# Softplus of the scans by a logistic function and squares on ACT, and an even spread of layer 0's scan groups

## The reference

```python
delta = jax.nn.softplus(jnp.einsum('er,brl->bel', dt_proj_w, dt_lo) + dt_proj_b[None, :, None])
def step(state, xs):
    d_t, B_t, C_t, u_t = xs
    dA = jnp.exp(d_t[..., None] * A)
    state = state * dA + (d_t * u_t)[..., None] * B_t[:, None, :]
    return (state, jnp.einsum('ben,bn->be', state, C_t))
```

## Time and profile before

| | us |
|---|---|
| median of 3 runs | 1293.16 |
| traced execution | 1297.12 |
| its span | 1295.4 |
| DVE busy in the span | 865.3 (67%) |
| POOL busy | 714.8 (55%) |
| PE busy | 1076.4 (83%) |
| ACT busy | 667.6 (52%) |

### The profile page before, as it was taken

How to read it: one execution, slowest core, us unless ns; L and a number is a source line. 1 busy time by engine, 2 the same in 40 slices (tenths; PEclk the granted TensorE clock), 3 DMA queues, 4 the chain that set the end, 5 groups by cost and what they waited for, 6 DMA issues and landing times.

```text
span 1295.4 us, 17796 instructions
## 1 busy us (share of the span) xinstructions
PE 1076.4 (83%) x5382; PEld 836.0 (65%) x5382; DVE 865.3 (67%) x1521; ACT 667.6 (52%) x1702; POOL 714.8 (55%) x480
## 2 busy tenths in 40 slices
PE   6576688778748878999999999798999737999992
PEld 3455577667514656888888888665555536887881
DVE  3885899878778975666656666769997772322221
ACT  4475355445462225778777777477652234333330
POOL 1106888888623223444454454439995206888873
PEclk8888799998968998999999999889999768999996
DMA  6494889986540003011101110304444983555555
GB/s 186 147 187 123 219 249 306 250 260 143 84 127 0 1 18 122 16 57 50 53 20 51 56 46 1 102 19 134 150 138 97 286 202 73 83 83 83 84 80 130
DMA packets 141119, 146.20 MB, mean 113 GB/s; under 512 B 34180, under 2 KB 127356, under 8 KB 141028
## 3 DMA queue, kind: packets, MB, share of 16 engines
q1 hardware_dynamic: 115556, 110.71, 29.5%
q0 software_dynamic: 24384, 33.31, 15.3%
q10 hardware_dynamic: 1088, 1.05, 0.2%
HBM read 119.04 MB, written 25.99 MB: 112 GB/s over the span
## 4 chain that ended last, share of the span: by engine, by line
PE 44%; POOL 18%; issue 14%; DVE 13%; DMA 6%; ACT 5%; another core or an unknown queue 0%; SPq 0%; ACTq 0%; POOLq 0%; DVEq 0%
PE bank L1629 4%; PE bank L1692 4%; PE bank L1725 4%; PE bank L1714 4%; POOL f_sums L1050 4%; POOL arena L1036 4%; PE bank L2491 3%; DMA f_sums<-arena,put 3%; POOL y L2407 2%; PE bank L1618 2%; PE bank L2159 2%; PE bank L1647 2%; PE bank L1703 2%; POOL arena L586 2%; DMA e_sums<-ctxT,put 2%
## 5 line engine op out<-in xcount | busy, mean ns | idle before, releaser
L566 DVE TENSOR_TENSOR_SCAN arena<-arena 128x1024 f32<-128x1024 f32 x64 | 155.2, 2425 | 15.4 <-issue 9.4
L1050 POOL DMA_INDIRECT f_sums<-arena,put x64 | 124.4, 1943 | 26.2 <-issue 17.1
L586 POOL TENSOR_TENSOR arena<-arena 128x1024 f32<-128x1024 f32 x32 | 82.5, 2577 | 89.6 <-DVE arena L566 89.6
L1036 POOL DMA_INDIRECT arena<-y_rows,slots x64 | 84.5, 1320 | 66.3 <-DVEq L1253 45.9
L2398 POOL DMA_INDIRECT e_sums<-ctxT,put x63 | 100.0, 1588 | 26.6 <-issue 16.2
L2491 PE MATMUL bank<-arena,ssm_y 128*128 x504 | 110.4, 363 | 0.9 <-issue 0.3
L544 ACT ACTIVATE arena<-arena,ssm_A 128x255 f32<-128x255 f32 x256 | 107.9, 499 | 1.1 <-DVE arena L488 0.9
L2159 PE MATMUL bank<-yT,arena 128*128 128x512 f32 (+1 forms) x224 | 104.3, 610 | 3.3 <-ACT arena L2090 3.3
L596 PE MATMUL bank<-arena,ident 128*128 128x256 f32 x256 | 68.7, 416 | 34.6 <-DVE arena L586 32.1
L2673 DVE TENSOR_SCALAR ctxT<-bank,slot_w 128x256 f32<-128x256 f32 x63 | 30.5, 484 | 99.1 <-DMA e_sums<-ctxT,put 89.5
L555 DVE TENSOR_TENSOR arena<-arena 128x1024 f32<-128x1024 f32 x64 | 94.3, 1473 | 0.2 <-DMA arena<-bc_rows 0.2
(11 more groups left out here) (342 smaller groups left out, 2777.1 us busy)
## 6 DMA issues: line engine op xcount, KB each, us to landing
arena<-bc_rows SPq DMA_DIRECT2D x64, 512.0 KB
arena<-in_L_ffn_w_gate_dram SPq DMA_DIRECT2D x16, 256.0 KB
arena<-in_L_ffn_w_up_dram SPq DMA_DIRECT2D x16, 256.0 KB
arena<-in_L_ffn_w_down_dram SPq DMA_DIRECT2D x16, 256.0 KB
x<-in_L_ffn_w_gate_dram SPq DMA_DIRECT2D x16, 256.0 KB
y<-in_L_ffn_w_up_dram SPq DMA_DIRECT2D x16, 256.0 KB
yT<-in_L_ffn_w_down_dram SPq DMA_DIRECT2D x16, 256.0 KB
arena<-in_L_ffn_Wd_dram SPq DMA_DIRECT2D x1, 3072.0 KB, 17.9
```

The lines of the kernel that those rows point to most:

```text
L566: nc.vector.tensor_tensor_scan(ssm_h[:, j % 2, :], ssm_decay[:, j % 2, :], ssm_in, 0.0, ALU.mult, ALU.add).then_inc(s_ssm_h, 1)
L586: ops.tensor_tensor(ssm_hC_buf[:, j % 2, :], ssm_h[:, j % 2, :], ssm_C[:, g % 2, :], ALU.mult).then_inc(s_ssm_hC, 1)
L1036: nc.gpsimd.indirect_dma_start(out=f0_xg[:, n % RING, e, :], out_offset=None, in_=y_rows, in_offset=bass.IndirectOffsetOnAxis(ap=slots[:, ...
L1050: nc.gpsimd.indirect_dma_start(out=f0_sums[m % SUMS], out_offset=bass.IndirectOffsetOnAxis(ap=put[:, m:m + 1], axis=0), in_=f0_ye[:, n % R ...
```

## The change

Softplus is computed another way. s is the logistic function: e / (2 + e) = sigmoid(-|z| - ln 2). The quartic in w is written as the product of two quadratics, each a square plus a constant: 2 atanh(s) = (du + near_add) x (t + 2 k far_add) x s, where du and t are squares that ACT makes of w with a bias from memory. ACT does Abs, Sigmoid and three squares for each block of 512 columns, DVE four operations for each half.

z goes through ACT once for all four blocks (`ssm_lin_act`, Identity with bias, followed by both products of u and D) ahead of the loop. The new `ssm_dt_act` then stands behind `silu(0)` for c = 0 and behind `silu(1)` for c = 1, each for two blocks. DVE's parts stand in pairs 1 and 2, and the groups from pair 3 on, one for each pair with a second one in pairs 3, 12 and 22. For the second scans `ssm_lin_act` comes ahead of the gate's Silu, ACT's blocks come in steps 0 to 3 of the feed-forward loop, DVE's parts in its steps 3 and 5, and `ssm_dt_done` in layer 2's attention.

```diff
+        def ssm_lin_act(act, m):
+            for c in range(HC):
+                for h in range(2):
+                    act.wait_ge(s_sp_dtp, 4 * m + 2 * c + h + 1)
+                    nc.scalar.activation(ssm_lin[:, c, h * HALF:(h + 1) * HALF], ssm_bank(2 * c + h)[:, :], ACT.Identity,
+                                         bias=ssm_par[:, 1, m, c:c + 1]).then_inc(s_sp_e, 1)
+            for c in range(HC):
+                nc.scalar.activation(ssm_y[:, m, :, c, :], ssm_u[:, c, :].rearrange("p (b l) -> p b l", b=B), ACT.Copy,
+                                     scale=ssm_par[:, 2, m, c:c + 1])
+
+        def ssm_dt_act(act, m, c, h):
+            cols = slice(h * HALF, (h + 1) * HALF)
+            lin, s, w = (z[:, c, cols] for z in (ssm_lin, ssm_e, ssm_w))
+            act.wait_ge(s_f0_const, 1)
+            act.wait_ge(s_sp_e, 8 * m + 4 + 2 * c + h)
+            act_link(nc.scalar.activation(s, lin, ACT.Abs))
+            act_link(nc.scalar.activation(s, s, ACT.Sigmoid, scale=-1.0, bias=soft_c[:, 0:1]))
+            act_link(nc.scalar.activation(w, s, ACT.Square))
+            nc.scalar.activation(ssm_du[:, c, cols], w, ACT.Square, bias=soft_c[:, 1:2])
+            nc.scalar.activation(ssm_delta[:, c, cols], w, ACT.Square, scale=math.sqrt(2 * SERIES),
+                                 bias=soft_c[:, 2:3]).then_inc(s_sp_e, 1)
...
+            dve.wait_ge(s_sp_e, 8 * m + 4 + 2 * c + 2)
+            dve_link(V.scalar_tensor_tensor(out=t, in0=t, scalar=2 * SERIES * far_add, in1=s, op0=ALU.add, op1=ALU.mult))
+            dve_link(V.scalar_tensor_tensor(out=t, in0=du, scalar=near_add, in1=t, op0=ALU.add, op1=ALU.mult))
+            dve_link(V.scalar_tensor_tensor(out=t, in0=lin, scalar=0.0, in1=t, op0=ALU.max, op1=ALU.add))
+            dve_link(V.tensor_tensor(du, t, u, ALU.mult))
...
+        f0_work = [[] for n in range(PAIRS)]
+        for c in range(HC):
+            f0_work[c + 1].append(("dt", 0, c))
+        for q in range(GROUPS):
+            f0_work[HC + 1 + q * (PAIRS - HC - 1) // GROUPS].append(("group", q // TURN, q % TURN))
...
             act.wait_ge(s_f0_clear, 16 * CLEARS)
-            ssm_dt_act(act, 0, 0)
+            ssm_lin_act(act, 0)
             step(0, 0, 0)
             for n in range(PAIRS):
                 if n + 1 < PAIRS:
                     step(n + 1, (n + 1) % RING, (n + 1) % 2)
                 silu(n, n % RING, n % 2)
-                if n == 0:
-                    ssm_dt_act(act, 0, 1)
+                if n < HC:
+                    for h in range(2):
+                        ssm_dt_act(act, 0, n, h)
                 if n:
                     evict(n - 1, (n - 1) % RING, (n - 1) % 2)
...
+                if i < 2 * HC:
+                    ssm_dt_act(act, 1, i // 2, i % 2)
...
-                for c, part in parts[2 + i:3 + i]:
-                    ssm_dt_part(dve, 1, c, part)
+                if i in (3, 5):
+                    ssm_dt_dve(dve, 1, (3, 5).index(i))
                 add(i)
...
-            ssm_dt_act(act, 1, 0)
+            ssm_lin_act(act, 1)
             gated_act(act, 0, 2)
-            ssm_dt_act(act, 1, 1)
             l1_act(act)
```

More of the change, by code:

```diff
@@ L462, in ssm_bc_sp, with ssm_dt_dve @@
                          x_dbl[DR:, :].rearrange("n (b l) -> n b l", b=B)).then_inc(s_sp_bc, 16)
-        def ssm_dt_dve(dve, m, c, part):
+        def ssm_dt_dve(dve, m, c):
             V = nc.vector
[L467 to L483, removed]
+            lin, s, t, du, u = (z[:, c, :] for z in (ssm_lin, ssm_e, ssm_delta, ssm_du, ssm_u))
+            dve.wait_ge(s_sp_e, 8 * m + 4 + 2 * c + 2)
[3 more added lines that the diff above has]
+            dve_link(V.tensor_tensor(du, t, u, ALU.mult))
+            if m == 0 and c == HC - 1:
                 ssm_dt_done(dve)
@@ L933, in flamingo_kernel @@
         s_f0_x = sem("s_f0_x")
-        f0_work = [[("dt", c, part) for part in range(3)] for c in range(HC)]
-        todo = [w for c in range(HC) for w in f0_work[c]] + [("group", q // TURN, q % TURN) for q in range(GROUPS)]
-        cost = [(6.5, 6.9, 3.7)[w[2]] if w[0] == "dt" else 4.75 for w in todo]
-        share, spent, f0_work = sum(cost) / PAIRS, 0.0, [[] for n in range(PAIRS)]
-        for n in range(PAIRS):
-            while todo and (spent + cost[0] / 2 <= share * (n + 1) or n == PAIRS - 1):
-                if f0_work[n] and todo[0][0] == "group" and todo[0][2] == 0 and n < PAIRS - 1:
-                    break
-                f0_work[n].append(todo.pop(0))
-                spent += cost.pop(0)
+        f0_work = [[] for n in range(PAIRS)]
[3 more added lines that the diff above has]
+            f0_work[HC + 1 + q * (PAIRS - HC - 1) // GROUPS].append(("group", q // TURN, q % TURN))
         f0_groups = [[w[1:] for w in work if w[0] == "group"] for work in f0_work]
@@ L1466, in add @@
                 norm_stats(dve, (i,), s_l1_x, i + 1)
-            parts = [(c, part) for c in range(HC) for part in range(7)][0:L1_PARTS]
-            for c, part in parts[0:2]:
-                ssm_dt_part(dve, 1, c, part)
             choose(0)
@@ L1928, in x_dve @@
             krms(0)
-            late = [(1, part) for part in range(L1_PARTS - 7, 7)]
-            for c, part in late[0:3]:
-                ssm_dt_part(dve, 1, c, part)
             qrms(0)
-            for c, part in late[3:]:
-                ssm_dt_part(dve, 1, c, part)
             ssm_dt_done(dve)
```

39 lines of the change are left out of this document (9 added, 30 removed).

## The result

The changed kernel takes 1306.2 us (median of 4, 1304.6 to 1307.9) where the kernel before takes 1293.0 beside it: ratio 1.0093, 95% interval 1.0064 to 1.0123. It is slower by 12 us (8 to 16). The forecast was 1292.4, with 1284 to 1300 around it.

A forecast was written before the change was run, and what follows sets the result against it. POOL's unbroken gathers and scatters were taken to bound layer 0's expert stage, DVE by busy share. Stage +1.2, gate -2.2, loop -1.0, Exp +1.3 sum to -0.7, giving 1292.4 us after subtracting the profiled run's 3.96 excess; range 1284 to 1300.

The forecast's parts named there:

- Late start, +6.5: Layer 0's expert stage: four softplus halves on ACT ahead of evict(0) make the first scatter 6.5 us later.
- First three pairs, +1.5: Layer 0, POOL: DVE's new operations and early scans make the first three pairs 7.9 us each, +1.5 us.
- Next 22 pairs, -2.1: Layer 0, POOL: fewer DVE operations holding POOL up over the next 22 pairs, -2.1 us, half of a possible -4.
- The tail, -4.7: Layer 0, closing scatters: the 4.68 us wait beside the last B and C loads goes, -4.7 us.
- Gate, -2.2: Layer 1's gate: Silu starts 2.2 us earlier, as its table load is no longer needed there.
- Loop, -1.0: Layer 1's feed-forward loop: DVE's softplus pieces cost 13.2 us in two lumps instead of 14.2, -1.0 us.
- Layer 2's first Exp, +1.3: Layer 2's attention: the first Exp needs a table load after the sigmoid set, +1.3 us.
- Rival 1: Layer 0: late first scatter is kept, POOL's tail gives nothing back; +4.0 us, 1297 (1299 with ACT's pause); chance 0.27.
- Rival 2: Layer 0: DVE's relief shortens POOL's pairs, 6.6 us beyond the sum, 1285.8; chance 0.31.
- Rival 3: ACT: Sigmoid, Tanh and Exp switch table sets, up to four more loads, 5 us, 1297.5; chance 0.04.
- the stage's upper bound: Layer 0's expert stage, summed at +1.2: +8 if the closing wait stays and nothing is won in between.

The follow-up runs named there:

- late_only: The kernel before plus only a delay: seven copies of 1.14 us on ACT ahead of evict(0); 1304.5 us, ratio 1.0071.
- l1_only: The kernel before with only the new softplus of the second scans (layer 1's loop), layer 0's stage as before; 1291.3 us, ratio 0.9978.
- spread_only: The kernel before with the old softplus and only the scan groups spread evenly over pairs 6 to 31; 1291.8 us, ratio 0.9983.
- after_again: The changed kernel as it is, measured and traced a second time; ratio 1.0071.
- exp_early: Changed kernel with ACT's blocks behind evict in pairs 0 to 3, DVE's second-softplus operations one by one, one early small Exp; 1286.6 us, ratio 0.9921.
- evict_first: The changed kernel with evict(n - 1) ahead of ACT's two blocks in pairs 0 and 1, nothing else; ratio 1.0029, repeated 1.0058.

## Why the prediction was wrong, point by point

**Late start, +6.5: right in mechanism, small in size.** Measured +7.1: the four blocks took 13.6 us and not 13.0 (from 113.46 to 129.12, less 1.28 for the load and 0.74 for the copy and Tanh between them). That POOL passes it on was right too, and late_only shows it alone: 8.25 us of delay made +6.4 at the first scatter (its trace has not the pause of 1.76) and 9 us in the time.

**First three pairs, +1.5: right.** 23.3 in both traces, 22.2 before: +1.1.

**Next 22 pairs, -2.1: wrong or too small to see.** 176.5 and 177.3, after 178.6 and 177.6: -1.2.

**The tail, -4.7: the step that failed.** I read the wait of 4.68 as the price of B and C rows beside the scatters, and took it as won whole. It did go, in all traces of the changed kernel. But the stretch from scatter 25 to the end is 31.8 in the mean where it was 32.8: -1.0. The groups that used to run while POOL waited now run beside the closing scatters, whose twelve durations sum to 23.8 and 25.0 where they were 21.8 and 20.9. The DVE timeline of the changed kernel beside the scatters of 341.13 and 346.64:

```profile
340.81 2.29 DVE L540 TENSOR_TENSOR_SCAN arena<-arena 128x1024 f32<-128x1024 f32 x1
...
346.32 2.29 DVE L540 TENSOR_TENSOR_SCAN arena<-arena 128x1024 f32<-128x1024 f32 x1
```

I had the rule for this myself, that scans hold POOL up, and didn't apply it to the moved groups. Nor is the wait tied to the order of the groups: l1_only has no such wait with the old order, and its last stretch is 30.5. spread_only has none either, and its stretch is 33.0, as long as before's with the wait. The Trainium skill (GPSIMD Engine Reference, Key points) gives that rule of the shared interface; the trace agrees with it once more (3.34 us beside each of the two scans above, 1.56 undisturbed).

**From the last scatter to the first sum: a term left out.** The prediction let everything behind the stage start when the last scatter has landed. ACT's own load of the third sum is a second path to the same point, as shown with the marks: 11.3 and 11.4 us after, 7.7 and 11.9 before, +1.5 in the mean. With such a spread in the kernel before, how much of it is the change's stays open.

**Gate, -2.2: right.** From the first sum of x to Silu 15.2 and 15.5 before, 13.0 and 12.4 after; over all traces the mean is 15.4 with the old gate (14.9 to 16.2) and 13.3 with the new one (12.0 to 15.2).

**Loop, -1.0: nearly right where PE's clock is the same.** The lumps of 6.6 us came as priced (rows below, the answer to the earlier trace rows).

```profile
450.59 1.21 DVE L482 SCALAR_TENSOR_TENSOR arena<-arena 128x1024 f32<-128x1024 f32 x1
451.83 2.83 DVE L483 SCALAR_TENSOR_TENSOR arena<-arena 128x1024 f32<-128x1024 f32 x1
...
455.96 1.22 DVE L485 TENSOR_TENSOR arena<-arena 128x1024 f32<-128x1024 f32 x1
```

From the first `add` to the last it is 65.6 us twice before, 67.5 and 65.0 after; the mean of the eight traces with lumps is 65.6, that of the five with the old loop 66.3: -0.7. From Silu to the last `add`, the stretch that the marks have, it is 104.8 twice before, 108.8 and 103.6 after. What sets these two apart is the speed of PE in the same program. PE's rows at the end of the loop, in the trace of 108.8:

```profile
466.03 1.97 PE L1372 MATMUL bank<-ident,arena 128*128 128x128 f32 x8 [3.55 <-POOL arena L1462]
...
485.66 1.84 PE L1372 MATMUL bank<-ident,arena 128*128 128x128 f32 x8 [2.84 <-POOL arena L1462]
488.67 5.68 PE L1379 MATMUL bank<-arena 128*128 128x256 f32 x16 [1.16 <-ACT arena L1402]
```

In after_again the last two took 1.09 us (behind a wait of 1.47) and 3.72, as before; and the loop's first product with the vectors took 7.13 us there, 9.46 in the trace of 108.8 (granted clock 0.50 from 403 to 407). Together that is 5.0 of the 5.2 us. The lumps don't bring the slow out-projection by themselves: six of the eight traces with lumps have 3.72, while two of the five with the old loop have 5.4 and all three with single operations 6.4 to 6.5, behind a wait of 2.36.

**Layer 2's first Exp, +1.3: right**, at the operation named (L1840, now L1809), on ACT's timeline, the answer to the earlier trace rows. From the last `add` to the second `x_kve` it is 31.7 and 30.6 after, 29.5 twice before.

```profile
521.12 1.28 ACT L1809 ACT_TABLE_LOAD   x1
522.41 0.56 ACT L1809 ACTIVATE arena<-bank,x_nb,x_rq 128x256 f32<-128x256 f32 x1
```

On the table load the trace stays with 1.28 us and the next operation at once, here and at 114.10. The Trainium skill's 1.38 us of drain on top (ScalarE: Activation LUTs, What ACT_TABLE_LOAD costs) isn't there.

**The rivals.** Rival 1, the late start kept, was the case, with 1297 for it where 1306 came: it kept the other gains. Its reason was off: the wait did go, and the closing scatters got longer instead. Rival 2 is out (mean scatter 1965 ns, gather 1313). Rival 3 is out: one load of the logistic set in layer 0 and one of Exp's at the first scan.

**The sum.** The marks give, in means of two traces each: start +7.1, first three pairs +1.1, next 22 -1.2, tail -1.0, first sum +1.5, gate -2.6, loop +1.4 and Exp with what follows +1.6, together +7.8 at the second `x_kve`, where the forecast had -0.7. The tail alone is 3.7 of the 8.5 us between them, the largest piece. From the first gather to the end of the span it is +5.9, so 2 us come back behind that mark; which of the later stages gives them, I didn't follow. The four traced executions themselves lie 6.9 us apart (1307.9 and 1300.0, 1297.1 and 1297.0). The timings say 9 to 12: after_again's trace is of the fastest of its six executions (median 1306.8), and the trace on which the forecast rests was 4 us slower than that kernel's median. So 2 to 5 us of the difference lie in executions of which there is no trace, and stay open.

The range was too narrow by its own terms as well: the stage's upper bound was +8, and with the gate and the loop at 0 and the Exp at 1.3 the bounds reach +9.3, 1302.5. Rival 1, on which the range ended, put the stage at +5.9, which is what the marks show at the end of the last scatter. The time of 1306 lies beyond even those bounds.

## What to carry to other kernels

What stands in a queue ahead of the first item of a saturated engine is paid about whole, whatever it relieves elsewhere: here the order of two calls on ACT was worth some 5 us, and a pure delay of 8 us on ACT cost 9. A wait that disappears is a gain only if what used to run inside it has another place; ask what each moved piece will run beside. And a consumer's work (DVE's scan groups) that starts as early as possible stands in front of the pipeline's own steps while these are still late: starting it one to two pairs later was worth 5 to 9 us. Last, where a stage ends with loads from two queues, look at both: the later one decides.

## What the runs showed of the hardware

PE's granted clock differs between executions of the same code. In layer 0's output projection, untouched by the change, PE's timelines show before and then after:

```profile
41.65 0.66 PE L753 MATMUL bank<-ident,arena 128*128 128x128 f32 x4 [2.04 <-DVE arena L828]
42.98 1.99 PE L764 MATMUL bank<-arena,yT 128*128 128x256 f32 x8 [0.68 <-ACT arena L803]
```

```profile
42.06 1.11 PE L727 MATMUL bank<-ident,arena 128*128 128x128 f32 x4 [2.05 <-DVE arena L802]
43.85 3.78 PE L738 MATMUL bank<-arena,yT 128*128 128x256 f32 x8 [0.68 <-ACT arena L777]
```

The gap ahead is the same (2.04 and 2.05 us), the eight matmuls take 1.99 us at 2.4 GHz and 3.78 at 1.2 (granted clock 1.00 and 0.50 from 44 to 48). PE's rows ahead of this gap (39.01 and 39.42) are 0.4 us apart in the two traces, those behind the product (46.09 and 49.43) 3.3, as the first gathers are; after_again, the same program, has 1.99 there. exp_early had its first gather at 101.90, behind a product of 3.78 in the same place, and the other traces at 97.0 to 98.6. The clock is also 5 us of what sets the two traces of the changed kernel apart (in the loop, above). It is not what sets apart those of the kernel before: the 4.2 us there lie between the last scatter and the first sum, where ACT loaded late.

The length of the gap doesn't tell it either. In evict_first the gate and up product of pair 2 stands behind 5.42 us of idle PE and takes 3.78 us, at a granted clock of 0.50, where it takes 1.95 to 1.96 at the full clock. But in the kernel before the same product takes 3.64 us, behind an idle stretch of 3.29.

```profile
118.78 3.78 PE L1072 MATMUL bank<-arena 128*128 128x128 f32 x16 [5.42 <-ACT arena L1131]
```
